# Weight rounding for the quantised feed-forward: the addend made by ScalarE in the middle chunks and by VectorE elsewhere

## What is computed

```python
def step(S, inp):                         # one chunk of 16 tokens
    kh = einsum('bchd,bhde->bche', ki, S)
    ...                                   # normalise, gradient, v_new
    o = qi + _ln(qh, w, b)
    S = S - einsum('bchd,bche->bhde', ki * ei[..., None], v_new)

def _quantized_matmul(x, w, scale):
    wq = w.astype(jnp.float8_e4m3fn).astype(x.dtype)
    return jnp.einsum('bsi,io->bso', x, wq) * scale
gate = silu(_quantized_matmul(x, gate_w, gate_scale))   # 512 -> 1536
up   = _quantized_matmul(x, up_w, up_scale)
y    = _quantized_matmul(gate * up, down_w, down_scale) # 1536 -> 512
```

## Time and profile before

| what | value |
|---|---|
| median of 3 runs | 873.86 us (873.23 to 876.57) |
| the profiled execution's own time | 873.76 us |
| its span in the trace | 872.0 us |
| TensorE matmul busy | 783.4 us (90%) |
| VectorE busy | 676.3 us (78%) |
| ScalarE busy | 498.4 us (57%) |
| GpSimd busy | 481.3 us (55%) |

### The profile page before, as it was taken

One profiled execution on the slowest core, in us unless ns is written; L12 is line 12 of the kernel. 1 busy time (PEld: TensorE's weight loads), 2 busy tenths in 40 slices (PEclk: granted clock), 3 DMA queues, 4 the chain that ended last, 5 costly groups with the idle time before them and its releaser, 6 DMA issues.

```text
span 872.0 us, 24457 instructions
## 1 busy us (share of the span) xinstructions
PE 783.4 (90%) x9068; PEld 594.6 (68%) x9068; DVE 676.3 (78%) x2704; ACT 498.4 (57%) x1328; POOL 481.3 (55%) x848
## 2 busy tenths in 40 slices
PE   8877777688978999999999999999999999978896
PEld 5655444476756777777768687776777777766695
DVE  3778887887878788878887888778887888868444
ACT  2776674767657565664657466656565565623331
POOL 5455746665555665646564656565565656545300
PEclk9998998888989999999999999999999999989998
DMA  8012120211201001000100010000100010001000
GB/s 278 26 50 61 37 63 25 74 38 29 65 30 38 15 2 50 2 26 2 50 2 27 2 39 14 26 2 2 50 2 26 2 50 2 2 2 49 1 25 25
DMA packets 16728, 28.58 MB, mean 33 GB/s; under 512 B 3521, under 2 KB 3521, under 8 KB 16609
## 3 DMA queue, kind: packets, MB, share of 16 engines
q1 hardware_dynamic: 16608, 27.02, 9.9%
HBM read 22.82 MB, written 4.19 MB: 31 GB/s over the span
## 4 chain that ended last, share of the span: by engine, by line
PE 62%; DVE 17%; POOL 9%; ACT 6%; issue 4%; SPq 1%; DMA 0%; POOLq 0%; DVEq 0%; ACTq 0%
PE bank L638 20%; PE bank L426 10%; PE bank L671 8%; PE bank L614 5%; PE bank L589 4%; POOL rho L1205 3%; PE bank L575 3%; PE bank L566 3%; PE bank L440 3%; PE bank L476 2%; DVE work L1517 2%; PE bank L460 2%; PE bank L597 2%; ACT BDq L953 2%; PE bank L454 1%
## 5 line engine op out<-in xcount | busy, mean ns | idle before, releaser
L1205 POOL TENSOR_TENSOR rho<-sy,cst 128x2 f32<-128x2 f32 x128 | 89.7, 701 | 221.6 <-DVE sy L1490 221.6
L589 PEld LDWEIGHTS bank<-VX,BDkR 128*64 128x64 f32 x1024 | 44.7, 138 | 81.6 <-issue 34.9
L589 PE MATMUL bank<-VX,BDkR 128*64 128x64 f32 x1024 | 56.2, 230 | 36.7 <-DVE VX L1526 36.0
L1533 DVE TENSOR_TENSOR SQ<-SQ,bank 128x128 f32<-128x128 f32 x128 | 36.5, 285 | 65.5 <-PE bank L589 64.6
L970 ACT ACTIVATE qhR<-bank 128x64 f32<-128x64 f32 x128 | 28.6, 223 | 101.5 <-PE bank L597 100.9
L929 ACT ACTIVATE BDkR<-kR,cst 128x128 f32<-128x128 f32 x256 | 81.6, 401 | 0.0
L671 PE MATMUL bank<-DW,fh 128*128 128x512 f32 x188 | 78.7, 419 | 0.6 <-DVE fl L1606 0.6
L915 ACT ACTIVATE BDk<-bank 32x256 f32<-32x256 f32 x124 | 46.5, 375 | 54.1 <-DVE kR L1432 45.8
L671 PE MATMUL bank<-DW,fl 128*128 128x512 f32 x188 | 74.6, 397 | 0.0
L566 PEld LDWEIGHTS bank<-SQ,BDk 128*64 128x64 f32 x1024 | 46.2, 140 | 40.7 <-issue 38.5
L1512 DVE SCALAR_TENSOR_TENSOR work<-work,rho,rR 128x32 f32<-128x32 f32 x256 | 53.1, 249 | 26.5 <-POOL rho L1205 26.3
(11 more groups left out here) (170 smaller groups left out, 2167.8 us busy)
## 6 DMA issues: line engine op xcount, KB each, us to landing
xt<-in_x SPq DMA_DIRECT2D x16, 256.0 KB, 2.9
x<-in_x SPq DMA_DIRECT2D x16, 256.0 KB, 3.0
out<-x SPq DMA_DIRECT2D x16, 256.0 KB, 2.1
yb<-in_gate_w SPq DMA_DIRECT2D x12, 256.0 KB, 2.7
yb<-in_up_w SPq DMA_DIRECT2D x12, 256.0 KB, 2.7
yb<-in_down_w SPq DMA_DIRECT2D x12, 256.0 KB, 2.7
Wk<-in_wk SPq DMA_DIRECT2D x1, 1024.0 KB, 6.7
Wv<-in_wv SPq DMA_DIRECT2D x1, 1024.0 KB, 8.4
```

The lines of the kernel that those rows point to most:

```text
L589: ins = mm(dS[p, e], bdkr[:, gh, j % 4, p], VX[:, e], start=True, stop=True, skip_group_check=True)
L1205: tt(dst, src, cst[:, C_NH:C_NH + n], ALU.pow).then_inc(*one)
```

## The change

In chunks 1 to 5 of blocks 0 to 4 (and in chunk 6 of blocks 0 to 2), VectorE's `exponent` at the end of the chunk before is left out. Instead ScalarE makes the absolute value of the weight times (2^20 - 4) straight from the staged weight, and its Relu then has scale 1. That is so for 25 of the 36 units; the other 11 go as before. ScalarE's steps for these units also stand elsewhere in its order: in chunk 1 behind `tail_xc`, in chunk 2 behind `ffn_fh`, in chunk 4 behind `post_osq`. The Abs waits for the staged weight and for the rounding of the unit before. The shift and the rounding stay as they are.

```diff
+STEEP = 2.0 ** 20 - 4
...
+        def by_scalar(u):
+            t, j = next((t, j) for t in range(NT) for j in range(NC) if u in unit_before(t, j))
+            return j in (1, 2, 3, 4, 5) or (j == 6 and early(t + 1))
+        def sized(u):
+            n = sum(by_scalar(m) == by_scalar(u) for m in range(u + 1))
+            return (s_size if by_scalar(u) else s_exp), n
...
-            def magic(u):
-                act.wait_ge(s_exp, u + 1)
-                if u == 0:
-                    act.wait_ge(s_eps, 7)
-                fn(wmg[:, :], wmg[:, :], ACT.Relu, scale=2.0 ** 20, bias=epses[:, 5:6]).then_inc(s_over, 1)
+            def magic(u, scale):
+                act.wait_ge(*sized(u))
+                fn(wmg[:, :], wmg[:, :], ACT.Relu, scale=scale, bias=epses[:, 5:6]).then_inc(s_over, 1)
                 act.wait_ge(s_over, u + 1)
                 fn(wmg[:, :], wmg[:, :], ACT.Identity, bias=epses[:, 6:7]).then_inc(s_magic, 1)
+            def from_exponent(t, j):
+                for u in unit_before(t, j):
+                    if not by_scalar(u):
+                        magic(u, 2.0 ** 20)
+            def from_weight(t, j):
+                for u in unit_before(t, j):
+                    if by_scalar(u):
+                        act.wait_ge(s_stage[u % 2], 16 * (u // 2 + 1))
+                        if u:
+                            act.wait_ge(s_quant, u)
+                        else:
+                            act.wait_ge(s_eps, 7)
+                        fn(wmg[:, :], wst[u % 2][:, :], ACT.Abs, scale=STEEP).then_inc(s_size, 1)
+                        magic(u, 1.0)
...
-                    for u in unit_before(t, j):
-                        magic(u)
+                    from_exponent(t, j)
...
                     if j == 1:
                         if tail and not s:
                             tail_xc(t - 2)
+                        from_weight(t, 1)
                         if scan:
                             diag_q(t, 1, s)
...
                     if j == 2:
+                        from_weight(t, 2)
                         if tail and not s:
                             tail_xf(t - 2, s, h - 1)
...
                     if j == 4:
                         if post:
                             post_osq(t - 1)
+                        from_weight(t, 4)
                         if scan:
                             diag_k(t, 3)
-                    if j == 5 and prep:
-                        prep_BDk(t + 1, o, 0)
+                    if j == 5:
+                        from_weight(t, 5)
+                        if prep:
+                            prep_BDk(t + 1, o, 0)
...
             def exponent(u):
+                if by_scalar(u):
+                    return
```

More of the change, by code:

```diff
@@ L181, in build @@
         s_stage = [sem(f"s_stage{n}") for n in range(len(wst))]
-        s_exp, s_over, s_magic, s_shift, s_quant = (sem(n) for n in ("s_exp", "s_over", "s_magic", "s_shift", "s_quant"))
+        s_size, s_exp, s_over, s_magic, s_shift, s_quant = (
+            sem(n) for n in ("s_size", "s_exp", "s_over", "s_magic", "s_shift", "s_quant"))
         s_mask = sem("s_mask")
@@ L1124, in body @@
                             prep_ksq(t + 1)
-                    if j == 3 and prep:
-                        prep_qT(t + 1, o)
+                    if j == 3:
+                        from_weight(t, 3)
+                        if prep:
+                            prep_qT(t + 1, o)
                     if j == 4:
@@ L1136, in body @@
                     if j == 6:
+                        from_weight(t, 6)
                         if prep and not early(t + 1):
```

## The result

The changed kernel took 869.71 us (median of 5 runs, 868.73 to 871.65) beside 873.86 for the kernel before: ratio 0.9937 [0.9919, 0.9956]. The two medians are 4.1 us apart (0.47%); the ratio says 0.63%, 5.5 us. The forecast was 871.5 in a range of 866 to 877: the time lies inside, but the gain is about twice the forecast one, and by both ratios over the 0.5% that I called the limit of what can be told from no change.

What follows compares the result with a forecast made beforehand. From 25 to 283 us the bound varies by chunk: VectorE's chain, TensorE's filler, or a path through ScalarE and GpSimd. 0.53 + 3.40 - 2.3 + 0.6 = 2.2 us off 873.76 gives 871.5, range 866.0 to 877.0.

Steps and rivals of the forecast that it cites:

- One exponent is worth 0.53 us on the chain: VectorE, from `quantize` to the next statistics: 1.13 us with the exponent, 0.60 without; ceiling about 13 us for 25.
- rival 4: ScalarE's Abs needs another table, two loads per unit, 64 us: up to 935 us; chance 0.02.
- What the update waited for is gained: Seven places leading into 0.3, 0.4, 1.2, 2.4, 3.5, 4.4, 4.5, where TensorE's update had waited for `VX`: +3.40 us.
- the gain through GpSimd's queue: A faster 3.2 frees GpSimd, whose queue ran without a gap to the power of 3.3: +0.53 us.
- Chunks 5 and 6 of blocks 0 to 2 lose 2.3: Six places where the Abs lengthens the path through ScalarE and GpSimd while VectorE's savings lie in its own wait: -2.3 us.
- Chunks 1 and 2 of blocks 2 and 4 gain 0.3 each: Four places: savings lost waiting for `ksq`, but GpSimd's shift runs without VectorE beside it; 0 to 0.4 a block, +0.6 us.
- Where the update had no idle time in front, nothing is gained: Eight places leading into a chunk where TensorE's filler sets the pace and ends no earlier: 0 us.
- the ledger: The prediction's gains and losses place by place over the 25 units, summing to +2.2 us.
- Rival 1: Fewer TensorE gaps let three early-stage fillers run at 2.4 GHz, 1.7 us each: 866.5 us; chance 0.23.
- My sign: TensorE's granted clock in blocks 1 to 3 rising above 0.92 would show that the clock comes up.
- Rival 3: A longer ScalarE queue delays `take_qh`, holding TensorE's query product, filler and update: 883 us, mildly about 876; chance 0.08.
- the inner range of 870.9 to 872.7: Forecast time with unknown terms at their ends: Abs of 0.72 in six full places, contention at 0 or 0.8.

Runs made afterwards that it cites:

- second experiment: Changed kernel, but in chunk 6 of blocks 0 to 2 VectorE makes the exponent again (three units): 867.83 us, 0.9916.
- seventh experiment: Changed kernel with ScalarE's Abs only in chunks 1 to 4, and in chunk 5 only of blocks 3 and 4: 866.52 us, 0.9896.
- third experiment: Changed kernel's order of ScalarE's Relu and Identity, but VectorE makes all 36 exponents and there is no Abs: 874.25 us, 0.9987.
- ninth experiment: Kernel before, with the change only in block 4 (five units, chunks 1 to 5): 871.85 us, 0.9966.
- sixth experiment: Changed kernel with a second Abs on ScalarE in each of the 25 units: 879.58 us, 1.0043.
- eighth experiment: Changed kernel with Abs only in chunks 1 to 4 (5 in blocks 3 and 4), plus useless matmuls filling TensorE's gaps: 868.42 us, 0.9911.
- The repetition: The changed kernel run once more, unaltered: 869.45 us, 0.9933 against the kernel before.
- its repetition: The kernel with Abs only in chunks 1 to 4 (5 in blocks 3 and 4), run again unaltered: 868.22 us, 0.9925.

## Why the prediction was right or wrong

- *One exponent is worth 0.53 us on the chain:* right, 0.61 us are left of 1.13. *The Abs takes 0.62 and a unit 0.65:* right, 0.622 and 0.64 to 0.67 from start to start. *No table load is added:* right, which takes rival 4 out.
- *What the update waited for is gained:* right. In the table 0.2-0.3 brings 0.96 of 1.06, 3.3-3.5 1.2 of 1.06 (with the gain through GpSimd's queue), 4.4-4.5 0.49 of 0.42.
- *Chunks 5 and 6 of blocks 0 to 2 lose 2.3:* right, -0.90, -0.83 and -0.67 make 2.4, and the second and seventh experiment show each Abs at its price. I had expected waits of 1.5 to 2 us before `prep_bx` in 0.6 and 1.6. 1.6 shows 2.06; in 0.6 it is 0.19, because VectorE there waits 3.61 us one step earlier, for the update, which stands behind a filler of TensorE that began after a wait of 1.46 us for `take_qh`. GpSimd's shift, 3.73 us late behind `magic`, ends at the same time: two paths that the Abs lengthened, not one.
- *Chunks 1 and 2 of blocks 2 and 4 gain 0.3 each:* near in block 2 (0.07), too low in block 4 (1.0). From the mark of 4.0 to `nb_f` of 4.2 it was 244.18 - 223.56 = 20.62 us and is 244.20 - 224.09 = 20.11. The shift starts 0.31 us later by that measure, behind `magic`, but takes 1.26 us instead of 1.64, and the `nm_f` behind it 0.19 instead of 0.64, since VectorE's operations have moved away: 0.83 where I had 0.4 at most. The other half is the exponent at the end of 4.2 (0.53), which I had at 0 because 4.3's update had no idle time in front. GpSimd in 4.2, first of the changed kernel:

```profile
241.94 1.26 POOL L1329 TENSOR_TENSOR yb<-x,yb 128x512 f32<-128x512 f32 x1 [2.35 <-ACT x L1033]
243.16 0.19 POOL L1245 TENSOR_TENSOR nm_f<-mv_f,epses 128x1 f32<-128x1 f32 x1
```

then of the kernel before:

```profile
241.10 1.64 POOL L1293 TENSOR_TENSOR yb<-x,yb 128x512 f32<-128x512 f32 x1 [1.18 <-DVE VX L1526]
242.70 0.64 POOL L1209 TENSOR_TENSOR nm_f<-mv_f,epses 128x1 f32<-128x1 f32 x1
```

- *Where the update had no idle time in front, nothing is gained:* this step failed, and it holds most of the error. I took the filler's length as given. In 4.3 that length was a product of the low clock, 1.05 us for four matmuls against 0.63. In 1.7 it was alike: sixteen matmuls of the projection took 5.25 us and the update did not wait, now they take 3.63 and it waits 1.45. In 2.3 twelve took 4.21 and now take 2.80. The third experiment parts the clock from the exponent: 1.8 of 4.3's 2.3 us and 0.8 of 2.3's 1.1 came with every exponent in its place. So what the exponents bring was sized rightly, and what I had at nothing is where the low clock falls. I put 1.7 (0.8), 1.0-1.1 (1.1) and 3.6-3.7 (0.5) down to the same cause, 4.9 us with 2.3's 0.8 and 4.3's 1.8, but only 4.3 was turned on and off by experiments; the rest is argued. Against it stands that 1.7 took 5.60 us in the ninth experiment without any change up to there, and that 1.0-1.1 is 0.4 over the ledger in one execution (11.40) and 1.8 in the other (9.99).
- *Rival 1, the clock comes up:* it had the mechanism and nearly the price (1.7 us for a filler before an update that doesn't wait; 1.8 measured in 4.3), but not the cause. I had looked for fewer gaps and set the gap ahead of the query product against it; in block 4 the kernels with that gap made longer are those with the low clock where it is hidden, the sixth and eighth experiment apart. My sign, a granted clock above 0.92 in blocks 1 to 3, came out at 0.93, 0.89 and 0.90 (0.87, 0.89 and 0.86 before), 0.91 in the mean. The repetition has 0.83 in block 1 with the same gain: the mean could not decide, the place did.
- *Rival 3, ScalarE becomes the bound:* not at one Abs a unit, but the sixth experiment shows it one step further, 1.0043 with two.
- *A smaller slip:* the inner range of 870.9 to 872.7 does not follow from its terms at the lower end. With the contention at 0.8 instead of 0.6 it is 871.3.
- *The start:* I had counted 0 ahead of chunk 0.1. Chunk 0.0 takes 1.0 us more in both executions after, but 4.51 us, as before, in the second experiment, and 5.17 in the ninth, where block 0 is unchanged; so it need not be the change's. The first mark lies at 29.31 and 27.82 us instead of 25.95 and 27.37; in the seventh experiment it is 25.62 and in its repetition 27.73. It varies from one execution to the next, and what of it the change makes is open, as is the 0.4 to 1.3 us behind 4.7. In the profiled execution TensorE waited 2.01 us for `Wk`'s transfer, and the projection then took 5.35 us, against 3.65 before:

```profile
10.59 5.35 PE L439 MATMUL bank<-Wk,xnT 128*64 128x512 f32 x16 [2.01 <-DMA Wk<-in_wk]
```

What stays open as well is what decides, ahead of a run, on which filler the low clock falls. The sixth and eighth experiment (4.3 at 7.07 us) have it on a part of the filler, the third (6.36) nowhere near, and 1.0-1.1 takes either 10.0 or 11.4 us in the same kernel. The best versions of those run are the second and the seventh, 0.9916 [0.9904, 0.9928] and 0.9896 [0.9874, 0.9918] (0.9925 [0.9911, 0.9938] in the repetition) against 0.9933 [0.9916, 0.9951] for the change. The intervals mostly overlap; what carries the claim is the 2.1 us in chunks 4 to 6 of blocks 0 to 2.

## What to carry to other kernels

Before a chunk is counted as bound by TensorE's filler, compare the duration of that filler with the same matmuls elsewhere: if it ran at the low clock, its length is no constant, and an edit on another engine can move the low clock to a place where a wait hides it, or back. Work moved from the engine on the chain to one beside it is free only where that engine has slack in the same chunk. Here the six places around chunks 5 and 6 had none, which the waits showed and the mean busy share (57%) did not, and taking the Abs away brought 0.4 to 0.8 us in 0.1, 2.0-2.2 and 4.0-4.2 too; at twice the cost more than half came through.

## What the runs showed of the hardware

- The same matmuls of TensorE took 1.7 times as long at the low clock (1.05 us for four against 0.63), and which of them do can change without any edit in front of them: 1.7 took 6.4 us twice and 5.60 once with the same program up to there.
- A longer wait of TensorE can go with a shorter chunk: with 2.13 us of idle time ahead of a projection that a wait hides, instead of 1.8 us twice behind it, 4.3 went from 8.15 to 5.83 us, of which 0.53 is the exponent. Filling gaps raised the granted clock from 0.87 to 0.96 in one stretch of 50 us, with no gain in time.
- GpSimd and VectorE slow each other. In 4.2, where they overlap, VectorE's 128x512 `fl` took 1.75 us, GpSimd's 128x512 shift 1.64 and its `nm_f`, of 128x1, 0.64; where they don't, after the change, 0.68, 1.26 and 0.19.
- The length of a chunk can take two values from one execution to the next (9.99 and 11.40 us), while most others repeat within 0.1 us.
